# Second attention of a four-layer kernel: rotation, rounding, remainder and stacking of a projection spread over successive quarters of a group

## The reference

```python
c_q = h @ w_down_q.T                  # h: x normed twice, with scale and bias
c_kv = h @ w_down_kv.T
q = (c_q @ w_up_q.T)                  # 16 heads of 64
k = (c_kv @ w_up_k.T)
v = (c_kv @ w_up_v.T)
q = _apply_rope_subspace(q, DR)       # e*cos - o*sin, e*sin + o*cos
k = _apply_rope_subspace(k, DR)
scores = einsum('bhqd,bhkd->bhqk', q, k) * scale
attn = softmax(scores, axis=-1)
out = einsum('bhqk,bhkd->bhqd', attn, v)
out = out @ w_out.T + residual
```

## Time and profile before

| | |
|---|---|
| median of three runs | 4091.57 us |
| profiled execution | 4099.89 us |
| its span | 4098.0 us |
| PE busy | 3758.8 us (92%) |
| POOL busy | 2664.7 us (65%) |
| DVE busy | 2409.3 us (59%) |
| ACT busy | 1690.9 us (41%) |

### The profile page before, as it was taken

How to read it: one execution, slowest core, us unless ns; L and a number is a source line. 1 busy time by engine, 2 the same in 40 slices (tenths; PEclk the granted TensorE clock), 3 DMA queues, 4 the chain that set the end, 5 groups by cost and what they waited for, 6 DMA issues and landing times. The chain is left out here.

```text
span 4098.0 us, 59114 instructions
## 1 busy us (share of the span) xinstructions
PE 3758.8 (92%) x16736; PEld 2513.8 (61%) x16736; DVE 2409.3 (59%) x2984; ACT 1690.9 (41%) x3212; POOL 2664.7 (65%) x1471
## 2 busy tenths in 40 slices
PE   2999999999999999978848999999999999999799
PEld 2666666666666666647735555556555556565488
DVE  4444444444444444436647777777777777777354
ACT  1344444444444444434413444444444444444254
POOL 2577777777777777742225667777777777777611
PEclk9999999999999999989969999999999999999899
DMA  5444444444444444210033444444444444443100
GB/s 174 106 102 102 100 101 103 103 103 103 103 103 103 103 102 100 57 34 31 31 89 90 92 99 93 93 94 94 93 99 99 99 99 98 96 96 74 44 19 26
DMA packets 312423, 363.63 MB, mean 89 GB/s; under 512 B 144544, under 2 KB 182304, under 8 KB 308256
## 3 DMA queue, kind: packets, MB, share of 16 engines
q1 hardware_dynamic: 303808, 291.43, 33.8%
q10 hardware_dynamic: 8544, 71.31, 4.9%
HBM read 138.68 MB, written 21.50 MB: 39 GB/s over the span
## 5 line engine op out<-in xcount | busy, mean ns | idle before, releaser
L863 POOL TENSOR_TENSOR b_rs<-b_rs,b_p 128x1024 f32<-128x1024 f32 x384 | 937.8, 2442 | 268.6 <-ACT b_p L776 250.1
L863 POOL TENSOR_TENSOR a_rs<-a_rs,a_p 128x1024 f32<-128x1024 f32 x384 | 915.0, 2383 | 287.6 <-ACT a_p L776 270.3
L790 DVE TENSOR_REDUCE a_nmax<-a_ps_x 128x1 fp32r<-128x1024 f32 x512 | 626.8, 1224 | 773.0 <-PE a_ps_x L605 770.5
L790 DVE TENSOR_REDUCE b_nmax<-b_ps_x 128x1 fp32r<-128x1024 f32 x512 | 626.0, 1223 | 331.5 <-PE b_ps_x L605 309.6
L776 ACT ACTIVATE b_p<-b_ps_s 128x512 f32<-128x512 f32 x1024 | 528.6, 606 | 415.6 <-PE b_ps_s L619 400.9
L776 ACT ACTIVATE a_p<-a_ps_s 128x512 f32<-128x512 f32 x1024 | 529.0, 604 | 400.0 <-PE a_ps_s L619 379.0
L605 PE MATMUL b_ps_x<-b_k,b_q 128*128 128x512 f32 x1024 | 406.2, 479 | 82.4 <-DVE b_nmax L790 68.8
L635 PE MATMUL b_ps_o<-b_p,b_v 128*64 128x512 f32 x2048 | 467.7, 598 | 0.0
L635 PE MATMUL a_ps_o<-a_p,a_v 128*64 128x512 f32 x2048 | 467.7, 598 | 0.0
L618 PE MATMUL b_ps_s<-b_q,b_k 128*128 128x512 f32 x1024 | 419.4, 410 | 30.4 <-ACT b_p L776 28.4
L605 PEld LDWEIGHTS b_ps_x<-b_k,b_q 128*128 128x128 f32 x1024 | 279.7, 316 | 249.4 <-issue 127.6
(11 more groups left out here) (166 smaller groups left out, 5919.9 us busy)
## 6 DMA issues: line engine op xcount, KB each, us to landing
a_k<-a_nat_h SPq DMA_DIRECT2D x256, 128.0 KB, 2.4
a_q<-a_nat_h SPq DMA_DIRECT2D x256, 128.0 KB, 2.4
b_k<-b_nat_h SPq DMA_DIRECT2D x256, 128.0 KB, 3.9
b_q<-b_nat_h SPq DMA_DIRECT2D x256, 128.0 KB, 3.4
feat<-feat_a ACTq DMA_DIRECT2D x15, 2048.0 KB, 9.0
feat<-feat_b ACTq DMA_DIRECT2D x15, 2048.0 KB, 10.1
a_k<-a_nat_l SPq DMA_DIRECT2D x128, 128.0 KB, 2.4
a_q<-a_nat_l SPq DMA_DIRECT2D x128, 128.0 KB, 2.4
```

The costliest lines, as they stand in the source:

```text
L790: dve.reduce_max(nmax[:, g % 2, head, qi:qi + 1], ps_x[:].rearrange("p a b -> p (a b)"), AX_X, negate=True).then_inc(s_red, 1)
L863: pool.tensor_tensor(out, out, p[:, bb, i, :], ALU.add).then_inc(s_sum, 1)
```

## The change

Only with `rope` (attention b), three things that were one step of the quarters 0 and 2 get places of their own. The rotation stays where it was. The rounding on ScalarE moves one quarter later (to the end of quarters 1 and 3). The remainder on VectorE moves two quarters later (quarter 2, and quarter 0 of the next window), and stands there directly behind the first reduce, ahead of `add_out` and `reciprocal`. On SyncE the stacking of n in even windows moves behind `spread` and the weight loads. The waits in front of `stack`, and the wait on `s_nat_l` between the two `sums_to_tile`, stand as they were; the semaphore's count n + 2 is now reached by a remainder of the next window.

```diff
-        def converted(u, b):
+        def rotated(u, b):
 
             return {0: 2 * u + 6, 2: 2 * u + 7}.get(b)
+
+        def rounded(u, b):
+
+            return rotated(u, b) if rope is None else {1: 2 * u + 6, 3: 2 * u + 7}.get(b)
+
+        def remainder(u, b):
+
+            return rotated(u, b) if rope is None else {0: 2 * u + 5, 2: 2 * u + 6}.get(b)
...
-                n = converted(u, b)
+                n = rounded(u, b)
                 if n is not None and live(t, 8, n, 4 * NPAIR):
                     convert_hi(act, t, n)
...
-                n = converted(u, b)
-                converting = n is not None and live(t, 8, n, 4 * NPAIR)
+                n, n_lo = rotated(u, b), remainder(u, b)
+                turning = rope is not None and n is not None and live(t, 8, n, 4 * NPAIR)
+                converting = n_lo is not None and live(t, 8, n_lo, 4 * NPAIR)
                 if live(t, 32, c, 8 * NGROUP):
                     reduce(dve, t, c)
+                if converting and rope is not None:
+                    convert_lo(dve, t, n_lo)
                 if b in (0, 2) and live(t, 4, u - 3, NGROUP):
                     add_out(dve, t, u - 3, b // 2)
...
-                if converting and rope is not None:
+                if turning:
                     rotate_odd(dve, t, n)
                 if live(t, 32, c + 1, 8 * NGROUP):
                     reduce(dve, t, c + 1)
-                if converting and rope is not None:
+                if turning:
                     rotate_even(dve, t, n)
-                if converting:
-                    convert_lo(dve, t, n)
+                if converting and rope is None:
+                    convert_lo(dve, t, n_lo)
...
-            if u % 2 == 0 and live(t, 8, n, 4 * NPAIR):
+            if u % 2 == 0 and rope is None and live(t, 8, n, 4 * NPAIR):
                 sp.wait_ge(s_nat_l, due(t, 8, n + 1))
                 stack(sp, n)
...
                 sp.dma_start(wv_r[:], w_v[source]).then_inc(s_wvr, 16)
+            if u % 2 == 0 and rope is not None and live(t, 8, n, 4 * NPAIR):
+                sp.wait_ge(s_nat_l, due(t, 8, n + 1))
+                stack(sp, n)
             if live(t, 4, u + 1, NGROUP):
                 sp.wait_ge(s_red, due(t, 32, 8 * (u + 2)))
                 shift(sp, u + 1, 0)
```

## The result

The changed kernel takes 4270.48 us (median of 4 runs, 4269.56 to 4272.1) against 4093.53 before on the same chip: the ratio is 1.043, interval [1.0412, 1.0448]. It is 177 us slower. I had forecast slower, but by 39 us, and the time lies outside my range.

The account below looks back on a forecast made before the run. Bound: TensorE's maxima in attention b waiting for VectorE's `reduce`. Losses of 6.4 + 0.3 + 0.4 + 4.5 = 11.6 us per body against 9.2 won, times 16 bodies, gave +39 on 4091.6: 4131 us, range 4030 to 4180.

Parts of the forecast that it names:

- The hold of the reciprocal: Even windows, quarter 0: second `sums_to_tile` waits for the remainder, delaying `reciprocal`; second reduce 2.7 late in window 0, 2.0 in window 2.
- A remainder costs the rest of GpSimd's instruction: VectorE waits until GpSimd's running add ends; a remainder costs between 0.7 and about 0.7 + 2.4 us.
- `add_out` covers only some 0.5 of it: Even windows, quarter 0: `reciprocal` waits until s + 6.5 (s the quarter's start), `add_out` filling about 0.5 us of that wait.
- hidden under 8.31 with it: 0.4 in all: Quarter 2: second reduce 0.1 to 0.4 late without v's projection, hidden by the 8.31 us quarter with it; 0.4 per body.
- The natural lengths: Undisturbed quarter lengths read from the timeline, such as 6.72, 4.52 and 4.62 us; a body takes 96.7 us.
- the pieces of q in window 0: Quarter 3: last piece lands at 26.8, 2.0 behind the feature load, for maxima due at 24.6; 2.2 us late.
- The 7.2 of the earlier trace: Time to landing taken for a small transfer issued beside the feature load, against 3.4 us ordinarily.
- meetings with GpSimd: Quarter 3, windows 1 to 3: `rot + turn` meets GpSimd's next adds; 0.8 us charged each, 2.3 together.
- Rival 1: The remainder finds GpSimd free and costs 0.7 us; 4.2 lost per body, -80 us, 4012 us; chance 0.25.
- Rival 2: Gain and price cancel: the reciprocal's 1.4 us hold in two windows is absorbed or shorter; 4085 us; chance 0.13.
- Rival 3: Pieces of q land late, at 29.0, in windows 0 and 2; +5.2 us per body, 4214 us; chance 0.06.
- Rival 4: Small transfers pass the feature load, so window 0's lateness for q shrinks to 0.6; 4105 us; chance 0.08.

Follow-up runs that it names:

- experiment 5: Changed kernel with attention b's remainder computed for 32 of 512 columns, leaving work out: 4145.02 us in one run.
- Experiment 1: Changed kernel with `add_out` put ahead of the remainder again on VectorE: 4173.6 us, ratio 1.0176 to the kernel before.
- experiment 3: Changed kernel with both edits, `add_out` ahead of the remainder and SyncE's wait moved out from between the two `sums_to_tile`: 4073.37 us, ratio 0.9929.
- experiment 2: Changed kernel with SyncE's wait for count n + 2 moved from between the two `sums_to_tile` to ahead of stacking n + 1: 4214.37 us, ratio 1.0275.
- experiment 4: Kernel of experiment 3 with window 0's feature load cut to 16 of 1024 columns, leaving work out: 3999.79 us, ratio 0.9752.
- experiment 6: Kernel before with only SyncE's edit, even windows' stacking of n behind `spread` and the weight loads: 4147.33 us, ratio 1.0129.
- experiment 10: Kernel of experiment 3 with the short chain kept around window 0, and the feature load issued behind ScalarE's move of v: 4047.55 us, ratio 0.9881.

## Why the prediction was wrong

**What held.** The hold of the reciprocal is there, 32 waits of VectorE for b_rq of 1.5 us each, where and for the reason given. Quarter 0 of window 0 is 2.8 longer than natural for a forecast of 2.7. A remainder costs the rest of GpSimd's instruction: mean 2.08, which experiment 5 confirms as a wait. ScalarE's waits for the rotation are gone. The direction was right.

**What failed first: the remainder moves all that stands behind it by 2.4, and I priced only the second reduce.** The prediction has "`add_out` covers only some 0.5 of it", and of quarter 2 "hidden under 8.31 with it: 0.4 in all". In both steps I took `add_out` as something that fills VectorE's time, and never asked who waits for it. Window 2 and 3's projection of v does, in quarters 0 and 2, and 0.3 us of slack is all that stood there: in window 3 before, `add_out` ended at 2788.36 and the projection began at 2788.70. In the table this is most of the 4.5 in quarter 2, where I charged 0.4, and, with the fall of the clock behind it, of the 3.8 in window 3's quarter 0, where I charged 0.5. In quarter 0 of window 2 it overlaps with the hold that I had charged. Experiment 1 puts it at 97 us with the hold in place; experiment 3 against 2 at 141 with the hold gone. Of the missing 138 us (177 less 39) it is the largest part. A line of the code before the change already said it: `pe.wait_ge(s_x, ...)` in `project_v`.

**What failed second: every loss was priced at the full clock.** Waits of 1.7 to 3.9 us are followed in many windows by products at half the clock: 5.35 for 3.65 in window 2, 6.0 for 4.52 in quarter 1 of window 0, and in quarter 3. The natural lengths that I added the waits to come from rows at full clock. The granted clock of attention b fell from 0.99 to 0.95; how much of the 177 us that is was not measured apart, but each fall costs 1.5 to 1.7 where it can be read. The mean clock sets a bound. Attention b after, then before:

```profile
2141.00:4010.00 1869.00, 1643.95 (x6506) 1015.72 (x6507) 1311.53 (x1314) 715.83 (x1393) 1243.09 (x652) 0.94 0.40 84
```

```profile
2142.00:3838.00 1696.00, 1585.45 (x6508) 984.86 (x6509) 1263.08 (x1313) 711.85 (x1393) 1225.53 (x652) 0.98 0.45 93
```

Six hundredths of 1869 us are 112, two of 1696 are 34; so at most some 80 of the 177 us are the clock, an estimate from these two rows. The gains of the experiments, too, include the falls that went with the waits.

**What failed third: the pieces of q in window 0**, charged with 2.2 and measured at a wait of 3.88, with 5.7 for the quarter of that body (6.1 in the table's). That the load makes them late was right. The pieces left 1.3 to 2.2 us later than I worked out, since quarter 1 ahead of them was slow by the clock and SyncE needed 4.7 instead of 3.7 us for the six, and from the last issue to the maxima it took 6.1 (2776.40 to 2782.50) where I had taken 5.0. The last piece landed 3.6 behind the load (11.0 and 5.9 to landing, so 2778.7 and 2782.3), not 2.0. The 7.2 of the earlier trace rows I had also misread: it is the middle of two pieces, one issued ahead of the load and one behind it. The kernel before, issues from 2717.3 to 2717.7 and from 2719.2 to 2719.7:

```profile
b_q<-b_nat_l SPq DMA_DIRECT2D x1, 128.0 KB, 4.1
```

```profile
b_q<-b_nat_l SPq DMA_DIRECT2D x1, 128.0 KB, 10.3
```

The load left at 2718.26 and took 10.7. So the piece issued 0.9 us behind the load landed about when the load did. In the changed kernel, where the pieces leave 5 us and more behind the load, they took 5.8 to 6.5. None took 7.2.

**What was charged too high.** In quarter 3 of windows 1 to 3 I charged 2.3 for meetings with GpSimd and 0.1 came; in quarter 0 of window 1 I charged 1.2 and 0.1 came, since the remainder took 1.36 there (at 2668.88) and not 2.4. These 3.3 us per body hid a part of what the three failures missed; that they did is luck.

**The rivals.** Rival 1 (GpSimd free) falls by the mean of 2.08; it came true in part in quarter 0 of window 1 alone. Rival 2 is experiment 2 turned round: the hold is real and worth 56 us. Rival 3 did not come, window 2 does not wait for q. Rival 4 falls by the two rows above and by experiment 4.

## What to carry to other kernels

When a step is put ahead of others on an engine, go through every semaphore that each of those others counts, and write down who waits for it and with what slack; the step that looks like filler may be the one with none. Two waits that hide each other must be removed together: here 97 and 56 us became 197, and turned a loss of 4.3% into a gain of 0.7%. And a transfer that is moved to the far side of a bulk load pays for the load even where the data it carries was ready in time (experiment 6). Last, check in the trace that an edit moved what it was meant to move: experiment 10's did not.

## What was not expected of the hardware

- A remainder of a sixteenth of the columns took 1.53 us on average instead of 2.17: what VectorE pays beside GpSimd's adds is mostly the other instruction's rest.
- The same wait of 1.72 us was followed by a fall of TensorE's clock in one body (16 products in 5.35 us) and by none in another (3.65 us), where the fall came one wait later, so a timeline of the kernel before cannot tell by itself what a new wait will cost.
- SyncE's issue of two stacking transfers, 1.23 us otherwise, took 1.96 beside the feature load.
